# Motif terms: each slab's neighbour planes gathered in two pieces of nine rows, over four shifts instead of two

## The reference, cut to what matters

```python
def _L1_conv_ref(feature):                    # (B, C=128 planes, 128, 96)
    ...                                       # Cg = 8 planes to a group, 9 shifted patches of each plane
    motif = patches.reshape(B, G, Cg * 9, L).reshape(B, G, 9, Cg, L)
    ...                                       # d2: distances from gram matrices
    nn_idx = jnp.argmin(d2, axis=-1)
    u_max = jnp.max(nn_idx, axis=-1)
    c_max = jnp.sum(nn_idx == u_max[..., None], axis=-1)
    motif_nn = jnp.take_along_axis(motif, u_max[..., None, None], axis=3)
    term = jnp.floor(motif * motif_nn * c_max[..., None, None] / Cg)
    out_ser = motif * batch_mask + term       # batch_mask is 0 for image 0
    ...                                       # each of the 9 terms is added back at its shift
```

## Time and profile before

| | us |
|---|---|
| median of 3 runs | 1623.61 (1621.33 to 1623.81) |
| the profiled execution's own time | 1614.49 |
| its span, first to last instruction | 1612.7 |
| `motif_terms` of image 0, in the span | about 512 to 803 |
| `motif_terms` of image 1, in the span | about 1317 to 1613 |
| DVE busy in these two stretches | 255.46 and 270.91 |
| PE busy in these two stretches | 251.21 and 250.59 |

### The profile page before, as it was taken

One profiled execution on the slowest core, in us unless ns is written; L12 is line 12 of the kernel. 1 busy time (PEld: TensorE's weight loads), 2 busy tenths in 40 slices (PEclk: granted clock), 3 DMA queues, 4 the chain that ended last, 5 costly groups with the idle time before them and its releaser, 6 DMA issues. The chain is left out here.

```text
span 1612.7 us, 33482 instructions
## 1 busy us (share of the span) xinstructions
PE 1313.7 (81%) x13401; PEld 1062.1 (66%) x13401; DVE 1139.1 (71%) x1813; ACT 852.4 (53%) x915; POOL 570.9 (35%) x619
## 2 busy tenths in 40 slices
PE   0799996995895789998868778878849958888988
PEld 0699986984885445555457768868849944454554
DVE  8577774567753798999855655753664338999998
ACT  0456552213440797888644444531125417888886
POOL 2688981552211201110056666824533112111000
PEclk9999997997997899999978989988979979999999
DMA  6376631962252716341145555317800327253411
GB/s 218 88 214 198 195 89 31 280 206 80 80 197 91 257 53 211 106 147 66 58 138 168 173 175 165 101 32 239 264 40 2 158 116 240 67 190 105 146 65 55
DMA packets 81791, 222.00 MB, mean 138 GB/s; under 512 B 16529, under 2 KB 20723, under 8 KB 78467
## 3 DMA queue, kind: packets, MB, share of 16 engines
q1 hardware_dynamic: 69540, 179.14, 34.7%
q0 software_dynamic: 4608, 27.49, 5.3%
q10 hardware_dynamic: 7488, 13.24, 3.0%
HBM read 101.98 MB, written 67.04 MB: 105 GB/s over the span
## 5 line engine op out<-in xcount | busy, mean ns | idle before, releaser
L1495 PE MATMUL acc<-rnd,ident 128*128 128x376 f32 x1152 | 405.2, 497 | 25.4 <-ACT rnd L1478 25.4
L1495 PEld LDWEIGHTS acc<-rnd,ident 128*128 128x128 f32 x1152 | 223.7, 198 | 153.1 <-ACT rnd L1478 26.8
L809 PE MATMUL ps_a<-wa,xa 128*128 128x192 f16 x1536 | 308.8, 253 | 14.3 <-DVE y_s L599 10.1
L809 PE MATMUL ps_a<-wb,xb 128*128 128x192 f16 x1536 | 307.4, 252 | 0.0
L1473 ACT ACTIVATE rnd_m<-prod,plus_round,scale 128x1504 f32<-128x1504 f32 x144 | 235.9, 1638 | 106.8 <-DVE prod L1322 97.4
L1322 DVE TENSOR_TENSOR prod<-fc,near 128x1504 f32<-128x1504 f32 x144 | 247.3, 1717 | 47.6 <-DMA near<-near 30.0
L1422 DVE SCALAR_TENSOR_TENSOR over<-prod,scale,rnd 128x1504 bf16<-128x1504 f32 x144 | 255.5, 1776 | 1.4 <-PE acc L1499 1.4
L533 POOL TENSOR_TENSOR vt<-z 96x256 f32<-96x256 f32 x248 | 249.1, 1024 | 18.7 <-ACT z L710 18.5
L1478 ACT ACTIVATE rnd<-rnd_m,minus_round 128x1504 f32<-128x1504 f32 x144 | 223.2, 1550 | 26.0 <-PE acc L1499 20.9
L809 PEld LDWEIGHTS ps_a<-wa,xa 128*128 128x128 f16 x1536 | 155.3, 101 | 21.2 <-issue 20.0
L809 PE MATMUL ps_a<-wfa,xa 128*128 128x96 f16 x1536 | 158.2, 208 | 13.4 <-DMA wfb<-qk 8.4
(11 more groups left out here) (256 smaller groups left out, 2261.0 us busy)
## 6 DMA issues: line engine op xcount, KB each, us to landing
xb<-xa ACTq DMA_DIRECT2D x64, 195.0 KB, 2.7
x_planes<-img SPq DMA_DIRECT2D x8, 1536.0 KB, 6.8
f_planes<-img SPq DMA_DIRECT2D x8, 1536.0 KB, 14.1
fc<-f_planes SPq DMA_DIRECT2D x16, 768.0 KB, 7.6
x1c<-x_planes SPq DMA_DIRECT2D x16, 768.0 KB, 6.7
out<-x1c SPq DMA_DIRECT2D x16, 768.0 KB, 4.5
v_a<-xa SPq DMA_DIRECT2D x40, 260.0 KB, 2.7
v_b<-xb SPq DMA_DIRECT2D x40, 260.0 KB, 3.2
```

The source lines that it names most:

```text
L809: mm = lambda a, w, first, end: nc.tensor.matmul(out(i), a, w, start=first and not opened, stop=end and not opened, skip_group_check=opened)
L1495: nc.tensor.matmul(o(m), k["ident"][:, :], rnd[:, n % RNDS, BR * m:BR * m + BR, :], start=False, stop=False, skip_group_check=True)
```

## The change

The gather of a slab of eighteen rows is made as two gathers of nine rows (`HALF`), for the slabs 2 to 7. Those of `near` are issued after the products of shifts 1 and 3, those of `near2` after the products of shifts 5 and 7. The slabs 0 and 1 are still gathered whole, before the first product. The index tile holds a second set of addresses, nine rows further on, which one more DVE instruction computes; the waits on `near_in` and `near2_in` count two landings for each slab from 2 on.

```diff
+    HALF = NR // 2
...
-        index = sb("index", [P, 2, N], I32)
+        index = sb("index", [P, 2, 2, N], I32)
...
+        landings = lambda i: 16 * sum(1 if j < 2 else 2 for j in range(i % SLOTS, i + 1, SLOTS))
...
-                eng.wait_ge(near_in[s], 16 * (i // SLOTS + 1))
+                eng.wait_ge(near_in[s], landings(i))
...
+        def part_run(i, h):
+
+            a, mid = run(i).start, run(i).start + HALF * C
+            return slice(a, mid) if h == 0 else slice(mid, run(i).stop)
...
-                        sp.wait_ge(near2_in[i % SLOTS], 16 * (i // SLOTS + 1))
+                        sp.wait_ge(near2_in[i % SLOTS], landings(i))
...
-            def gather(i, second):
+            def gather(i, second, cells, h=0):
                 s = i % SLOTS
                 pool.indirect_dma_start(
-                    (near2 if second else near)[:, s, run(i)], None, f_dram.rearrange("y (e o) -> (y e) o", o=1),
-                    bass.IndirectOffsetOnAxis(ap=index[:, second, i:i + 1], axis=0)
+                    (near2 if second else near)[:, s, cells], None, f_dram.rearrange("y (e o) -> (y e) o", o=1),
+                    bass.IndirectOffsetOnAxis(ap=index[:, second, h, i:i + 1], axis=0)
                 ).then_inc((near2_in if second else near_in)[s], 16)
...
             for second in range(2):
-                gather(0, second)
-                gather(1, second)
+                gather(0, second, run(0))
+                gather(1, second, run(1))
+            pool.wait_ge(indexed, 2)
             for n, (i, sh) in enumerate(steps):
-                if sh in (1, 3) and i + 2 < N:
+                if sh in (1, 3, 5, 7) and i + 2 < N:
                     product_made(pool, n)
                     if sh == 1 and i + 2 == N - 1:
                         nc.gpsimd.memset(near[:, (i + 2) % SLOTS, R * C:NR * C], 0.0).then_inc(edged, 1)
-                    gather(i + 2, sh // 2)
+                    h = sh // 2 % 2
+                    gather(i + 2, sh // 4, part_run(i + 2, h), h)
...
-            nc.vector.tensor_tensor(index[:], offset[:, :].unsqueeze(2).to_broadcast([P, 2, N]),
-                                    k["row_base"][:, :].unsqueeze(1).to_broadcast([P, 2, N]), ALU.add
-                                    ).then_inc(indexed, 1)
+            for h in range(2):
+                nc.vector.scalar_tensor_tensor(index[:, :, h, :], offset[:, :].unsqueeze(2).to_broadcast([P, 2, N]),
+                                               float(HALF * C * h),
+                                               k["row_base"][:, :].unsqueeze(1).to_broadcast([P, 2, N]), ALU.add,
+                                               ALU.add).then_inc(indexed, 1)
```

## The result

| | before | after |
|---|---|---|
| median of the timed runs, us | 1622.95 (1621.33 to 1623.81) | 1601.80 (1600.58 to 1602.17) |
| ratio after to before | | 0.9879, 95% interval 0.9856 to 0.9902 |
| span of the profiled execution, us | 1612.7 | 1599.9 |
| first product to last `finish`, image 0 and image 1, us | 279.4 and 282.5 | 263.9 and 275.3 |

The account below looks back on a forecast made before the run. DVE's pace and its stalls on late moves were taken to bound the kernel. Of 26.2 us of stalls, 5.4 would stay; the 20.8 us gain, cut to 20.5 for PE waits, gave 1603 us, own range 1599 to 1609, 8-in-10 range 1597 to 1616.

Parts of the forecast that it names:

- The bound: In `motif_terms`, DVE sets the pace at 3.33 us a step; its stalls on late moves are lost for good.
- waits for PE: 1.0 and 0.3 us in the two images; may grow by a few tenths when stalls no longer hide them.
- the first moves: The first stall in each image, 2.73 and 2.39 us, stays, behind the whole gathers of slabs 0 and 1.
- The relief of a group: Steps 5 and 6, or 9 and 10: two half gathers fewer ahead shrink a group's stalls by 2.6 us, not below zero.
- What is taken out of the backlog comes out of the landing: At steps 5, 6, 9 and 10, transfers ahead start no earlier or later, so less backlog means the last move lands earlier.
- all stalls go: Rival, chance 0.12: smaller blocks let the moves of steps 9 and 10 slip between; 26 us go, 1597 us.
- The late halves: `near2`'s half gathers at shifts 5 and 7 delay moves by at most 1.45 us, with 2.7 to spare; taken as nothing.
- slower, by the late halves: Rival, chance 0.06: each late half delays a move as a whole gather delays step 5; 45 us lost, 1648 us.
- The smaller pieces: A half gather, with descriptors of 3.46 KB where they were 6.9, takes 1.45 us of the DMA engines.
- POOL and the new landings: 24 more gathers of 2.24 us on POOL are hidden, and the second halves land in time; both taken as nothing.
- A half one in a quiet queue stays below that: `near2`'s second half lands in less than a whole gather's 7.1 to 12.6 us, with 13.3 us before SP waits.
- products longer than 1.72 us: Named sign of being wrong: DVE's products growing beyond their 1.72 us.

Follow-up runs that it names:

- halves_same_shift: Against the kernel before: each gather in two halves, both issued at the shift where the whole one was; 1610.75 us, ratio 0.9945.
- whole_1_and_5: Against the kernel before: whole gathers, `near`'s at shift 1 as before, `near2`'s at shift 5 instead of 3; 1611.60 us, ratio 0.9945.
- changed_side_by_side: The changed kernel unchanged, timed again on one chip beside the one with a mark behind each late gather; 1601.86 us, ratio 0.9899 to the kernel before.

## Why the prediction was right, and where it wasn't

*The bound.* DVE's pace of 3.33 us a step and its stalls on moves set the stage. This held: thirteen of sixteen stalls went and three shrank to tenths, and the stretches shortened by what they had cost. By the rows, 24 us of idle and some 1 us of restarts went, 1.4 us came back as waits for PE, and 0.6 us more stood at the first moves: 23 us, against 22.8 by the stretches.

*The relief of a group, 2.6 us: too small.* This term was made from the queue's bytes and its mean rate. The group with the most left over, steps 9 and 10 of the first pair, was to keep 1.9 us and kept 0.3 with the restart (0.19 of idle); all groups together were to keep 5.4 us and kept 1.2 (1.0 of idle). The gauge says why: the landing of the move of step 10 fell by 4.2 us, from 9.4 to 5.2. The term counts the bytes of two half gathers, and 0.90 MB fewer of gathers were indeed moved ahead of this move. What it leaves out is the 0.73 MB of SP's own queue. A rate that is a mean over sixteen DMA engines counts the bytes, but a move waits for the last of its parts, and with shorter gathers less of what stands behind it overtakes this last part. The picture drawn from the earlier trace rows, a gather served almost in one piece while SP's queue waits, came from 3 us and is only part of it: over the 9.4 us of this move SP's queue held 63.2% of the engines and the gathers' 38.9%. The landing of a gather itself comes nearer to the 4.2 us: 7.1 us at the shortest, and 5.1 with half the rows, so 2.0 us for a half, and 4 for two. That is one case, and no run shows that the two go together elsewhere.

*"What is taken out of the backlog comes out of the landing": only part of it.* The sum had it that halving does nothing until bytes are moved to later shifts. Halving alone gave 14.6 of the 22.8 us by the stretches (9.0 us by the medians), and moving `near2`'s whole gathers to shift 5 gave about what the sum would have said, 13.0 us by the stretches and 8.2 by the medians. What halving alone gives is nearest to the mechanism of the rival "all stalls go", smaller blocks between which the moves get through. Why halves at the same shift do so much is settled only so far: less of SP's own queue goes ahead of the move's last part. Both of these are in them: a half is a shorter block, and POOL starts on the second half 1.7 to 2.6 us after the first, so that it arrives later. No run parts the two.

*The late halves, taken at nothing:* right for the moves. Steps 12, 13, 16 and 17 land in 2.0 to 3.6 us, and even whole gathers there stall none of these moves. The rival "slower, by the late halves" fell.

*The smaller pieces:* taken a little too dear. The prediction gave a half 1.45 us where half of a whole is 1.38. The gathers' queue went from 5.3% to 5.4% of the span, and its line on the page after says more:

```profile
q0 software_dynamic: 4992, 27.50, 5.4%
```

These are 4992 packets where there were 4608, for 24 gathers more: a whole gather is 144 packets and a half 80, 6.1 and 5.5 KB each on average. So the pieces did not shrink to one half, from 6.9 to 3.46 KB, as the prediction had it, and the packets of the other queue were no guide to their price. The fixed cost of a transfer that the prediction cites from the Trainium skill (DMA: Bandwidth & Descriptors, the fit in the section on the anatomy of one DMA) does not show as time that the engines are held.

*POOL and the new landings, taken at nothing:* wrong in some executions. "A half one in a quiet queue stays below that" left out that POOL may not get to write it. In one of three profiles of the changed kernel this cost 6.67 us. The row of before that I leant on, 2.24 us for a gather on POOL and 2.25 at the most, was taken in a kernel whose DVE still stalled. One more sign of being wrong had been named, products longer than 1.72 us. The changed kernel's first profile hardly shows it (1.715 us on average, 1.73 at most); its two repeats have 1.728 and 1.729 us on average, with single ones up to 1.76. Over 288 instructions that is an estimated 3 us, and whether the change brings it isn't known.

So the time was right to 0.1%, and not all of it for the right reason. The relief was taken 4 us too small, and 1.4 us of waits for PE and 0.6 us at the first moves were hardly in the sum, so the stretches gained 22.8 us where 20.5 were forecast. The medians gained 21.15 us, and in the later rounds 14.3 and 16.6 us. The closeness is in part luck: the stages that the change doesn't touch took 10 us more in the profile after than in the one before, which is far more than the 1.2 us between forecast and result. Caught gathers explain a part of the smaller gains, but only the profiled executions have traces, so that is argued and not shown. Of the rivals, "all stalls go" is nearest to what the trace shows; it was priced at 1597 us, and the fastest execution of the changed kernel, in a later round, took 1595.39.

## What to carry to other kernels

Price a transfer that blocks others by the landings of what stands behind it, not by bytes over the queue's mean rate alone. Before splitting a transfer and moving the pieces, try each alone: here halving alone, and moving one of the two gathers alone, gave about half each, and moving both whole gathers to the quiet shifts took away every stall without any splitting. And when the last stalls of a busy DVE go, look at the longest instruction on POOL: a gather may live on those stalls. A mark behind it, on which DVE waits a few steps later, held the loss to 1 us in both cases seen.

## What the runs showed of the hardware

An indirect DMA's instruction on POOL can be held up for long while DVE runs f32 instructions with two inputs from SBUF back to back. Its length was 0.94 us where DVE was idle, 2.25 us at the most in the kernel before, 3.0 and 3.9 us often after, and 8.91 to 42.61 us in the ten caught gathers. Of the ten, nine ended 0.81 to 0.83 us after the last instruction before a stop of DVE. The tenth, of 10.55 us, ended 0.83 us after the end of an instruction while DVE ran on, and so, with some 0.8 us, did all gathers of 2.25 to 3.9 us. It looks as if a gather gets through at the change from one DVE instruction to the next, mostly at the first or second, and a caught one misses 4 to 28 of them; that is read off the times and was not tested. Caught gathers were seen in eight of the thirteen profiled executions of other kernels than before's, all of them with few or no other stalls left, and in none of before, `halves_same_shift` and `whole_1_and_5`, which stall often. What starts it isn't known.

DVE's products beside a caught gather took 1.75 to 1.78 us against 1.72. But products of up to 1.76 us are in `changed_side_by_side` too, which has no caught gather, so the length alone is no sign of a lockout.

The Trainium skill describes such a lockout (SBUF — State Buffer, section on the two sides of SBUF, the note on the "DVE blocks DMA" trap): GpSimd can't write the descriptors of a DMA that it issues while DVE holds the port that they share. It gives it for DVE's two-port modes; here the instructions are TENSOR_TENSOR and SCALAR_TENSOR_TENSOR in f32. The same page (section on who interferes with whom) infers that tensor_tensor leaves the writing of descriptors alone, but says that a DVE instruction with two SBUF inputs contends with a GpSimd instruction that reads SBUF. A gather here reads its addresses from `index` in SBUF, so by the second rule it could be held. No run tells whether the reading or the writing is held up.
